# A cross attention's sixteen heads regrouped: two heads' scores at once, sums and mixes of four heads in strips

## The reference, cut to what matters

```
q = x @ Wq                      # 128 -> 16 heads of 64
k, v = split(context @ Wkv)     # 77 rows, 16 heads of 64 each
sim  = einsum('bhid,bhjd->bhij', q, k) * 64 ** -0.5
sim  = where(mask, sim, -max)
sim  = clip(sim, -5, 5)
attn = softmax(sim)             # over the 77 context rows
out  = einsum('bhij,bhjd->bhid', attn, v)
return out (heads side by side, 1024 wide) @ Wo + bo
```

## Time and profile before

| | us |
|---|---|
| median of 3 runs (lowest, highest) | 5019.0 (5018.72, 5026.54) |
| the profiled execution's own time | 5025.06 |
| its span in the trace | 5023.3 |
| PE busy, share of the span | 4148.4 (83%) |
| DVE busy | 2535.3 (50%) |
| ACT busy | 1577.9 (31%) |
| mean granted clock of PE | 0.913 |
| first matmul of the stage to the next norm's residual add, first pass | 67.07 (871.58 to 938.65) |

### The profile page before, as it was taken

How to read it: one execution, slowest core, us unless ns; L and a number is a source line. 1 busy time by engine, 2 the same in 40 slices (tenths; PEclk the granted TensorE clock), 3 DMA queues, 4 the chain that set the end, 5 groups by cost and what they waited for, 6 DMA issues and landing times. The chain is left out here.

```text
span 5023.3 us, 96105 instructions
## 1 busy us (share of the span) xinstructions
PE 4148.4 (83%) x38100; PEld 2542.9 (51%) x38100; DVE 2535.3 (50%) x6018; ACT 1577.9 (31%) x3504; POOL 789.6 (16%) x1372
## 2 busy tenths in 40 slices
PE   6997787978799778787879977878787997787878
PEld 3873343454487334345548733435454873343544
DVE  4664534544566443454456644335445764443544
ACT  3442222432344222243234422224323442222431
POOL 1430001110143010011014301001102420100110
PEclk7999998989799999898979999989897999999989
DMA  1001000000000100000000010000000001000000
GB/s 75 4 3 54 17 13 3 21 29 28 24 3 3 54 18 14 1 21 33 24 24 3 2 54 18 14 1 21 33 24 24 3 12 45 18 14 1 21 33 26
DMA packets 11010, 104.56 MB, mean 21 GB/s; under 512 B 1148, under 2 KB 5552, under 8 KB 6192
## 3 DMA queue, kind: packets, MB, share of 16 engines
q1 hardware_dynamic: 10544, 98.17, 5.1%
HBM read 97.12 MB, written 1.05 MB: 20 GB/s over the span
## 5 line engine op out<-in xcount | busy, mean ns | idle before, releaser
L88 PE MATMUL psum<-ident_bf 128*128 128x512 bf16 x1896 | 528.8, 419 | 201.1 <-DVE l_attn_peak L770 67.3
L88 PEld LDWEIGHTS psum<-ident_bf 128*128 128x128 bf16 x1896 | 187.1, 106 | 480.5 <-issue 173.2
L2730 DVE TENSOR_TENSOR l_attn_xx<-l_attn_xx,psum 128x256 f32<-128x256 f32 x512 | 205.9, 419 | 215.1 <-PE psum L2459 203.0
L2562 ACT ACTIVATE l_attn_ax<-psum 128x128 f32<-128x128 f32 (+1 forms) x768 | 184.7, 278 | 361.2 <-PE psum L2440 245.6
L399 DVE TENSOR_TENSOR l_ffn_hidden<-l_ffn_silu,psum 128x512 f32<-128x512 f32 (+2 forms) x184 | 126.0, 686 | 320.7 <-ACT l_ffn_silu L340 320.4
L94 PEld LDWEIGHTS psum<-streamed_weights,l_ffn_hidden 128*128 128x128 f32 (+2 forms) x1728 | 226.4, 192 | 117.8 <-issue 100.0
L340 ACT ACTIVATE l_ffn_silu<-psum 128x512 f32<-128x512 f32 (+2 forms) x216 | 128.8, 596 | 472.3 <-PE psum L310 471.9
L2455 PE MATMUL psum<-l_attn_ax,l_attn_xx 64*64 64x64 f32 x5120 | 268.2, 224 | 0.0
L2459 PE MATMUL psum<-l_attn_xx,l_attn_ax 64*64 64x64 f32 x5120 | 261.1, 221 | 0.0
L770 DVE TENSOR_REDUCE l_attn_peak<-psum 128x4 f32<-128x2048 f32 (+3 forms) x128 | 185.6, 1487 | 122.4 <-PE psum L688 121.5
L2628 POOL TENSOR_TENSOR l_attn_part<-l_attn_ab,streamed_weights 128x128 f32<-128x128 f32 x640 | 241.7, 410 | 27.4 <-PE psum L2440 27.4
(11 more groups left out here) (501 smaller groups left out, 8397.9 us busy)
## 6 DMA issues: line engine op xcount, KB each, us to landing
streamed_weights<-pack_l_ffn SPq DMA_DIRECT2D x4, 5412.0 KB, 16.4
streamed_weights<-pack_l_ffn SPq DMA_DIRECT2D x4, 3972.0 KB, 13.8
streamed_weights<-pack_l_attn SPq DMA_DIRECT2D x5, 2848.5 KB, 9.6
streamed_weights<-pack_l_xattn SPq DMA_DIRECT2D x4, 2496.0 KB, 8.9
streamed_weights<-pack_l_ffn SPq DMA_DIRECT2D x4, 2192.0 KB, 8.6
streamed_weights<-pack_l_xattn SPq DMA_DIRECT2D x4, 2048.0 KB, 8.5
streamed_weights<-pack_l_ffn SPq DMA_DIRECT2D x4, 1667.5 KB, 7.3
streamed_weights<-pack_l_attn SPq DMA_DIRECT2D x4, 1107.5 KB, 5.2
```

The source lines that it names most:

```text
L88: pe.matmul(self.bank(bank), self.ident_bf[:, :], self.ident_bf[:, :].unsqueeze(1).to_broadcast([P, NT, P]), start=True, stop=True)
L2562: act.activation(ax[b, p, :, :], m.psum[b, p, 0:P].rearrange("p (i t) -> p i t", i=2), ACT.Copy).then_inc(ax_ready, 1)
L2730: dve.tensor_tensor(both, both, m.psum[:, p, P:384], ALU.subtract).then_inc(x_less, 1)
```

## The change

`stage_l2_xattn` is written anew. Heads go through it in four groups of four (two pairs each).

- k and v are kept without padding: ACT copies k (two copies, after the K matmuls), DVE copies v (two copies), and the clear of `v` is gone.
- The two heads' scores of a pair are two matmuls, one on the rows 0 to 63 and one on the rows 64 to 127 of `k` and `q`, into two PSUM banks. One clip and one exponential take both banks (77x1024), in place of two each of 77x512.
- The sums of four heads are four matmuls of 32 columns of ones, one for each set of 32 output partitions, into bank 4. One reciprocal of 128x512 serves the four heads.
- The mixes are two sets of four such matmuls: features 0 to 31 of the four heads into bank 5, 32 to 63 into bank 6. Each set is multiplied by the same reciprocal, and projected; `wo` is packed in this order of rows.
- `q` has four buffers, `prob` four (the clip writes into them, the exponential works in place). Queries use banks 4, 5 and 7, each when it is free.
- The order on the engines is written out anew.

```diff
-    W, J = 64, 8
+    W, J, G, Q = 64, 8, 4, 32
...
+                def score(j):
+                    pe.wait_ge(q_ready, j + 1)
+                    if j == 0:
+                        pe.wait_ge(k_ready, 2)
+                    if j >= 2:
+                        pe.wait_ge(clip_ready, j - 1)
+                    for half in range(2):
+                        rows = slice(W * half, W * half + W)
+                        ins = pe.matmul(m.psum[0:S2, 2 * (j % 2) + half, :], k[rows, j, :], q[rows, j % 4, :],
+                                        start=True, stop=True)
+                    ins.then_inc(scores, 1)
+
+                def sums(g):
+                    pe.wait_ge(prob_ready, 2 * g + 2)
+                    if g == 0:
+                        pe.wait_ge(q_ready, 3)
+                    if g >= 1:
+                        pe.wait_ge(rec_ready, g)
+                    if g == 2:
+                        pe.wait_ge(q_ready, 7)
+                    for c in range(4):
+                        ins = pe.matmul(m.psum[quad(c), 4, :], m.const["ones"][0:S2, 0:Q],
+                                        prob[:, (2 * g + c // 2) % 4, c % 2, :], start=True, stop=True)
+                    ins.then_inc(sums_psum, 1)
+
+                def mix(g, n):
...
+                    for c in range(4):
+                        ins = pe.matmul(m.psum[quad(c), 5 + n, :], v[:, 4 * g + c, Q * n:Q * n + Q],
+                                        prob[:, (2 * g + c // 2) % 4, c % 2, :], start=True, stop=True)
+                    ins.then_inc(mix_psum, 1)
...
+                query(0, 4)
+                query(1, 7)
+                score(0)
+                score(1)
                 for n in range(2):
...
+                    pe.matmul(m.psum[0:S2, 5 + n, :], m.ctxT[:, :], w["wv"][:, n, :], start=True,
+                              stop=True).then_inc(v_psum, 1)
+                query(2, 4)
+                score(2)
+                query(3, 7)
+                for g in range(G):
+                    sums(g)
+                    if 2 * g + 3 < J:
+                        score(2 * g + 3)
+                    mix(g, 0)
+                    mix(g, 1)
+                    if g == 0:
+                        pe.wait_ge(q_ready, 4)
+                        query(4, 7)
+                        pe.wait_ge(q_ready, 5)
+                        query(5, 7)
+                    else:
+                        project(g - 1, 0)
+                        project(g - 1, 1)
+                    if g == 1:
+                        pe.wait_ge(rec_ready, 2)
+                        query(6, 4)
+                    if 2 * g + 4 < J:
+                        score(2 * g + 4)
+                    if g == 1:
+                        pe.wait_ge(mixed_ready, 3)
+                        query(7, 5)
+                project(G - 1, 0)
+                project(G - 1, 1)
...
+                act.wait_ge(k_psum, 1)
+                for n, (a, b) in enumerate(((0, 6), (6, 8))):
+                    act.activation(k[:, a:b, :], m.psum[:, 5 + n, 0:(b - a) * S2].rearrange("p (j s) -> p j s", s=S2),
+                                   ACT.Copy).then_inc(k_ready, 1)
+                query(0, 4)
+                query(1, 7)
+                exponential(0)
+                query(2, 4)
+                exponential(1)
+                query(3, 7)
+                exponential(2)
+                query(4, 7)
+                query(5, 7)
+                exponential(3)
+                exponential(4)
+                query(6, 4)
+                exponential(5)
+                query(7, 5)
+                exponential(6)
+                exponential(7)
...
+                clip(0)
+                clip(1)
+                for n in range(2):
+                    dve.wait_ge(v_psum, n + 1)
+                    dve.tensor_copy(v[:, 8 * n:8 * n + 8, :],
+                                    m.psum[0:S2, 5 + n, :].rearrange("p (h d) -> p h d", d=W)).then_inc(v_ready, 1)
+                clip(2)
+                for g in range(G):
+                    reciprocal(g)
+                    if 2 * g + 3 < J:
+                        clip(2 * g + 3)
+                    divide(g, 0)
+                    divide(g, 1)
+                    if 2 * g + 4 < J:
+                        clip(2 * g + 4)
...
-            ("wv", g("Wkv")[:, 1024:].reshape(P, 2, 512)), ("wo", tiles_of(g("Wo")))]
+            ("wv", g("Wkv")[:, 1024:].reshape(P, 2, 512)), ("wo", g("Wo").reshape(4, 4, 2, 32, P).transpose(1, 3, 0, 2, 4).reshape(P, 8, P))]
```

More of the change, by code:

```diff
@@ L1010, in stage_l2_xattn @@
     nc, w, name = m.nc, m.weights("l2_xattn"), "l2_xattn"
-    W, J = 64, 8
+    W, J, G, Q = 64, 8, 4, 32
     limit = 5.0 * W ** 0.5
+    quad = lambda c: slice(Q * c, Q * c + Q)
     with ExitStack() as ctx:
@@ L1029, in stage_l2_xattn @@
         prob_ready = sem("prob")
-        pair_psum = sem("pair")
+        sums_psum = sem("sums")
+        rec_ready = sem("reciprocal")
+        mix_psum = sem("mix")
         mixed_ready = sem("mixed")
         out_done = sem("out")
-        chain_sem = sem("chain")
         with nc.Block(no_gpsimd_drain=True) as block:
@@ L1050, in score @@
-                def score(h):
-                    pe.wait_ge(q_ready, h // 2 + 1)
-                    if h >= 2:
-                        pe.wait_ge(clip_ready, h - 1)
-                    pe.matmul(m.psum[0:S2, 5 + h % 2, :], k_heads[:, h, :], q[:, (h // 2) % 2, :],
-                              start=True, stop=True).then_inc(scores, 1)
-                def mix(h):
-                    j, half = divmod(h, 2)
-                    pe.wait_ge(prob_ready, h + 1)
-                    if half == 0 and j >= 2:
-                        pe.wait_ge(mixed_ready, j - 1)
-                    a = 2 * (j % 2)
-                    pe.matmul(m.bank(a), v[:, j, half, :], prob[:, h % 3, :], start=half == 0, stop=half == 1)
-                    pe.matmul(m.bank(a + 1), m.const["halves"][0:S2, half, :], prob[:, h % 3, :],
-                              start=half == 0, stop=half == 1).then_inc(pair_psum, 1)
@@ L1067, in project, with query @@
-                def project(j):
-                    pe.wait_ge(mixed_ready, j + 1)
-                    m.project(pe, mixed[:, j % 2, :], w["wo"][:, j, :], j == 0, j == J - 1).then_inc(out_done, 1)
-                query(0)
-                pe.wait_ge(kv_ready, 1)
-                for h in range(H + 6):
-                    if h % 2 == 0 and h // 2 + 1 < J:
-                        query(h // 2 + 1)
-                    if h < H:
-                        score(h)
-                    if 2 <= h < H + 2:
-                        mix(h - 2)
-                    if h >= 6 and h % 2 == 0 and (h - 6) // 2 < J:
-                        project((h - 6) // 2)
+                def query(j, bank):
+                    pe.matmul(m.bank(bank), w["wq"][:, j, :], m.xnT[:, :], start=True, stop=True).then_inc(q_psum, 1)
@@ new lines, in project @@
+                def project(g, n):
+                    pe.wait_ge(mixed_ready, 2 * g + n + 1)
+                    if g + n == 0:
+                        pe.wait_ge(q_ready, 6)
+                    m.project(pe, mixed[:, g % 2, n, :], w["wo"][:, 2 * g + n, :], g + n == 0,
+                              g + n == G).then_inc(out_done, 1)
+                for j in range(J):
+                    ins = pe.matmul(m.psum[:, 5 + j // 6, (j % 6) * S2:(j % 6 + 1) * S2], w["wk"][:, j, :],
+                                    m.ctxT[:, :], start=True, stop=True)
@@ L1083, in _, with query @@
+                project(G - 1, 0)
+                project(G - 1, 1)
             @block.scalar
             def _(act):
[L1085 removed]
+                def query(j, bank):
                     act.wait_ge(q_psum, j + 1)
[L1087 to L1099 removed]
+                    if j >= 4:
+                        act.wait_ge(scores, j - 3)
+                    act.activation(q[:, j % 4, :], m.bank(bank), ACT.Copy).then_inc(q_ready, 1)
@@ L1125, in _, with clip @@
-                ins.then_inc(kv_ready, 1)
-                for h in range(H + 3):
-                    if h < H:
-                        dve.wait_ge(scores, h + 1)
-                        if h >= 2:
-                            dve.wait_ge(prob_ready, h - 1)
-                        dve.tensor_scalar(clipped[:, h % 2, :], m.psum[0:S2, 5 + h % 2, :], -limit,
-                                          m.bound[:, :], ALU.max, ALU.min).then_inc(clip_ready, 1)
-                    if h >= 4 and h % 2 == 0:
-                        quotient(dve, chain, h // 2 - 2)
+                def clip(j):
+                    dve.wait_ge(scores, j + 1)
+                    if j >= 4:
+                        dve.wait_ge(mix_psum, 2 * (j // 2 - 1))
+                    dve.tensor_scalar(prob[:, j % 4, :, :], m.psum[0:S2, 2 * (j % 2):2 * (j % 2) + 2, :], -limit,
+                                      m.bound[:, :], ALU.max, ALU.min).then_inc(clip_ready, 1)
```

82 lines of the change are left out of this document (31 added, 51 removed).

## The result

The changed kernel takes 4956.93 us (median of 4 runs, 4951.96 to 4957.86) beside 5022.77 us for the kernel before on the same chip: ratio 0.9865, 95% interval 0.9848 to 0.9882. In a second set it was 4953.65 us, ratio 0.9861 (0.9834 to 0.9887). On the scale of the 5019.0 us forecast upon, 0.9865 is 4951 us. The forecast was 4931 us in a range of 4914 to 4955: faster, as said, by 68 us and not 88, inside the range but outside the likeliest case's own, 4916 to 4944. It is inside by a part of the range that was added for two rivals, and neither of them came. The interval of the ratio is 4943 to 4960 us on that scale and so reaches past the upper end; the median in its own microseconds, 4956.93, lies there too.

A forecast was written before the change was run, and what follows sets the result against it. PE was taken to bound the stage (60.27 of 66 us); the new chain of 42.2 us against 64.12 saves 21.9 us per pass, 87.6 in four, from 5025.06 to 4937.5, on the median's scale 4931 us, range 4914 to 4955.

The forecast's parts named there:

- the likeliest case: The forecast itself, 4931 us with its own bounds 4916 to 4944, chance 0.78.
- two rivals: Double scores taking 1.72 us (4952 us, chance 0.08); one slow-clock stretch per pass in the stage (4944 us, chance 0.09).
- PE side by side: Strips and 64-row halves on PE run side by side: strips 0.88 us, a double score 0.86.
- The rival's price: Double scores take 1.72 us, not 0.86; six on the chain, 5.2 us per pass, total 4952; chance 0.08.
- Changes of shape: On PE, each switch between full, strip and half matmuls costs 0.15 us, bounds 0 and 0.3; eleven on the chain.
- The chain: Changed stage, first K matmul to start of last project: 42.2 us against 64.12, 21.9 less per pass.
- Group 2: Third group's link of the chain, bound by DVE and ACT, 7.0 us; PE's mixes and projects, 5.2 us, fit beside it.
- Elementwise work: Larger DVE and ACT pieces: clip 1.29 us, exponential 1.06, reciprocal 3.35, multiply 0.69, k's copies 0.56 and 0.31.
- The clock in the stage: PE's granted clock in the changed stage stays at 0.99.
- clock rivals: Changed stage partly at the slow clock (4944 us, 0.09), or wholly (5069 us, 0.03 together with shape changes eating the gain).
- The cover in group 0: Pair 3's clip, behind the reciprocal on DVE, ends 5.7 us after the sums, exponential wanted at 7.4: 1.7 us cover.
- The mis-sized term: Stages behind the changed one start earlier against the clock's slow stretches and may shift a few us either way.

The follow-up runs named there:

- the serial run: Changed kernel with k padded by zero rows to 128, so a pair's two scores run one after another: 4957.66 us, stage 57.10 us.
- the reciprocal more: Changed kernel with a second DVE reciprocal ahead of each: 5013.95 us, stage 64.53 us.
- the shifts: Unused matmuls behind the last project: changed kernel with 5, 10, 15, span +6.5, +1.5, +13.6 us; kernel before with four, +18.6 us.
- the other order: Changed kernel with three queries moved in PE's list, their copies beside other matmuls: 4951.74 us, stage 49.27 us.
- the two lengths within one kernel: Changed kernel with each reciprocal taken twice, 5013.95 us: stage behind 186.88 us in the first two passes, 190.20 in the last two.
- with 128 rows: Feed-forward's 4-row matmuls widened to 128 rows by zeros: 4927.57 us (0.9808) in the changed kernel, 5039.27 us in the kernel before.
- an edit of +21.6 us in its stage: Changed kernel with k padded by zeros so that scores run one after another: 4957.66 us.
- one of -9.8 us: Changed kernel with three queries moved in PE's list: 4951.74 us beside the changed kernel's 4953.65.

## Why the prediction was right, and where its 20 us went

- **PE side by side.** Right: strips 0.88, double score 0.86 (1.02 with the change of shape behind it), against 1.87 when serial. The rival's price of 5.2 us per pass stands beside 5.4 in the serial run, which has two copies more and some changes of shape less.
- **Changes of shape.** Right: 0.09 to 0.16 where 0.15 was taken; one from a query to strips (880.91 to 881.96) 0.19. By the Trainium skill ("TensorEngine Tiling (Array Packing)", Key Properties) such a change drains TensorE. The trace agrees that it isn't free and makes it small: eleven cost 1 to 2 us of 51.7.
- **The chain.** Forecast 11.1, then 8.6, 9.4, 7.0 and 6.1 to the last project; measured 11.1, 8.4, 9.5, 6.7 and 6.2. Group 2 is bound by DVE and ACT as said. To the next add it is 44.38 us where about 45 stood, because the tail behind the last project is 2.4 us, not 2.95: before, that project ran at the half clock (1.72 against 1.05), which the prediction had among its bounds. So 22.7 us a pass against 21.9, 90.8 against 87.6.
- **Elementwise work.** Clip 1.24 on the mean (1.29 forecast), exponential 1.05 (1.06), reciprocal 3.36, multiply 0.68, DVE 29.1 us in the stage (30.6). The exception is k's two copies, 0.74 us together against 0.87; the line through the prediction's own two rows gives 0.55 and 0.29, not 0.56 and 0.31. PE's busy time, 39.1, isn't the 35 forecast: "busy" counts the changes of shape, 1 to 2 us, and the tails of about 0.2 us that stand uncovered ahead of each of the seven waits, 1.4 us. About 1 us stays unexplained.
- **The clock in the stage.** Right: 1.00 throughout, so neither of the clock rivals came in the stage. With gaps of 1.85 and 4.03 us they did (the reciprocal more).
- **The cover in group 0.** Right: the clip behind the reciprocal ended at 887.55, and its exponential began 1.75 us later, at 889.30, behind a query's copy.

**The mis-sized term** is the sentence "Stages behind start earlier against the clock's slow stretches and may shift a few us either way". They shifted 22.6 us one way: 12.0 in the feed-forward stage behind, 10.6 elsewhere. Without it the sum would have said 5025.06 - 90.8 = 4934; with it the execution took 4957.1. The prediction had named a test, that it is wrong if other stages take back or add more than 10 us, and by this test it was wrong in that term. That the time still fell inside the range is luck: the range reached to 4955 for serial scores and a slow stretch in the stage, and what filled it was something else. The runs now let the trace of before be read better: that feed-forward stage met its slow stretch 1.2 us after its 4-row matmuls had begun, and it was 183.0 us where all other kernels with 4-row matmuls have 184.8 to 190.2. So before was at the good end for such kernels and a shift could mostly lose, which its own trace alone didn't show. Its row of the spread in 4.39 us, only partly slow, was there to read. A term of 2 to 5 us a pass with one sign for this one stage (an estimate made after the runs, from 184.8 to 188.5 less 183.0) would have been nearer; "a few us either way" for four passes wasn't enough.

What the runs show of the cause: where the slow stretches fall sets the length of the stage behind, with its code unchanged (the shifts, the other order, the two lengths within one kernel), and with 128 rows the fall at this place goes in both kernels. What stays open: whether the begin of the stage or PE's work ahead of it moves the falls; the 10.6 us in the other stages, mostly the first layer's attention (no run acted on it, though its passes took 368.2 to 377.0 us in these kernels behind the first pass), and what decides where, after a slow stretch is removed, the next one falls.

## What to carry to other kernels

Forecast a stage by its chain of starts, and price an operation on the stage's own length, not on the total: here an edit of +21.6 us in its stage left the total unmoved, and one of -9.8 us as well. Where TensorE's clock falls in stages that the change doesn't touch, give each saving its own uncertainty for where they land, some 5 us per pass for a stage that has such stretches (an estimate from the 181.6 to 190.2 us of the stage behind), and ask whether before is at the lucky end. Then look at what PE does when the clock falls. Widening the matmuls over few rows at that place was worth more in the changed kernel (27 to 29 us, by 0.9808 against 0.9861 and 0.9865 of 5019) than the next reordering of the chain, but only 16 us of that came in its own stage, and in the kernel before it was worth nothing.

## What the hardware showed beyond the expected

- TensorE's granted clock fell to 0.50 while it was fully busy: in the changed kernel no gap stands between 933.54 us and the fall between 938.70 and 938.80. By the Trainium skill ("TensorE: Matmul & The Clock Gate", What's actually happening) the gate follows how busy the engine has been; the trace agrees for the kernel with a reciprocal more, where the fall to 0.50 at 910.5 us came behind 4.03 us of waiting. Busy time alone doesn't tell the two kernels here apart: with 4 rows PE was busy for 5.16 of the 5.20 us before the fall, and with 128 rows in eight of those matmuls, the same columns and the same list, it was busy for 5.28 of 5.30 us (932.10 to 937.40) and the clock held. Which property of the 4-row matmuls counts, and whether those behind the fall had a part, no run shows.
- Rows cost no time themselves: at 1.00 the 4-row matmuls of L1697 stand 0.99 us from start to start (935.72 to 936.71), over 128 rows 1.00 us (934.29 to 935.29). The four of 384 columns take 2.85 us over 128 rows at 1.00, and 5.48 over 4 rows at 0.50; that difference is the clock.
- A slow stretch is long (3.5, 6.8 and 10.2 us in the rows above), and where the stretches fall moved the stage behind, with its code unchanged, between 183.0 and 190.2 us, by 3.3 us even between two passes of one kernel.
